# An MLP written out at both ends: the branch on odd weights first, eight PSUM banks, the last output layer tile by tile

## What is computed

```python
def _tlin(x, w, s): return jnp.einsum('bsi,oi->bso', x, w) * s   # w holds -1, 0 and 1
# x is 8 x 256 x 128; w1, w2: 512 x 128; h1, h2: 512 x 512; w3: 128 x 512
h = silu(_tlin(x, w1_w, w1_s)) * _tlin(x, w2_w, w2_s)
h = gelu(_tlin(h, h1_w, h1_s), approximate=False)
h = gelu(_tlin(h, h2_w, h2_s), approximate=False)
x = _layernorm(x + _tlin(h, w3_w, w3_s))
```

## Time and profile before

| what | value |
|---|---|
| three runs | 384.06, 384.48, 386.58 us; median 384.48 |
| the profiled execution | 384.94 us |
| its span, first to last instruction | 383.1 us |
| mean granted TensorE clock | 0.963 of full speed |
| TensorE busy | 334.1 us, 87% |
| DVE, ACT, POOL busy | 263.8, 210.9, 180.4 us |

### The profile page before, as it was taken

One profiled execution on the slowest core, in us unless ns is written; L12 is line 12 of the kernel. 1 busy time (PEld: TensorE's weight loads), 2 busy tenths in 40 slices (PEclk: granted clock), 3 DMA queues, 4 the chain that ended last, 5 costly groups with the idle time before them and its releaser, 6 DMA issues.

```text
span 383.1 us, 8611 instructions
## 1 busy us (share of the span) xinstructions
PE 334.1 (87%) x2572; PEld 305.8 (80%) x2572; DVE 263.8 (69%) x849; ACT 210.9 (55%) x429; POOL 180.4 (47%) x242
## 2 busy tenths in 40 slices
PE   3798899976857999999967999999688999999991
PEld 1798788866747999988856888888588999999890
DVE  3767877866853578678863989887865777666641
ACT  2457556624522455455466878875357666767330
POOL 0033777655472447975687666643133333233300
PEclk9999999976896999999998999999999999999997
DMA  8980001021232625223303000000000000000000
GB/s 270 432 331 0 23 29 37 31 62 35 56 79 71 199 58 169 56 62 86 109 24 125 0 2 2 1 3 2 1 2 3 0 15 15 14 14 3 27 14 17
DMA packets 17033, 23.71 MB, mean 62 GB/s; under 512 B 3424, under 2 KB 14176, under 8 KB 16208
## 3 DMA queue, kind: packets, MB, share of 16 engines
q1 hardware_dynamic: 13712, 17.97, 14.3%
q0 software_dynamic: 2272, 4.69, 3.7%
q10 hardware_dynamic: 1008, 0.53, 0.5%
HBM read 17.45 MB, written 6.73 MB: 63 GB/s over the span
## 4 chain that ended last, share of the span: by engine, by line
PE 61%; DVE 9%; issue 8%; POOL 4%; ACT 3%; another core or an unknown queue 2%; POOLq 0%; DVEq 0%; ACTq 0%
PE ps L1902 8%; PE ps L1903 8%; PE ps L1539 7%; PE ps L1541 6%; PE ps L1540 6%; PE ps L1739 5%; PE ps L1943 3%; PE ps L1847 3%; PE ps L1728 2%; PE ps L1862 2%; PE ps L1622 1%; POOL sb_w_lo L568 1%; ACT sb_stage L724 1%; PE ps L1874 1%
## 5 line engine op out<-in xcount | busy, mean ns | idle before, releaser
L1902 PE MATMUL ps<-sb_w_hi,sb_fh_hi 128*128 128x256 f32 x256 | 63.5, 286 | 0.9 <-POOL sb_w_lo L596 0.8
L1903 PE MATMUL ps<-sb_w_lo,sb_fh_hi 128*128 128x256 f32 x256 | 62.7, 283 | 0.0
L1902 PEld LDWEIGHTS ps<-sb_w_hi,sb_fh_hi 128*128 128x128 f32 x256 | 49.0, 191 | 1.3 <-POOL sb_w_lo L596 1.0
L1903 PEld LDWEIGHTS ps<-sb_w_lo,sb_fh_hi 128*128 128x128 f32 x256 | 49.0, 191 | 0.0
L596 POOL TENSOR_TENSOR sb_w_lo<-sb_x_in,sb_w_hi 128x256 fp32r<-128x256 f32 x32 | 23.3, 759 | 43.2 <-DVE sb_w_hi L1484 43.2
L448 POOL DMA_INDIRECT routed<-sb_rows_of,sb_row x32 | 31.8, 993 | 17.6 <-issue 9.1
L1739 PE MATMUL ps<-sb_w,sb_stage 128*128 x234 | 34.1, 284 | 3.9 <-ACT sb_xT_in L730 3.0
L1539 PE MATMUL ps<-sb_w_hi,sb_rT_hi 128*128 x78 | 30.6, 392 | 7.2 <-issue 5.0
L1739 PEld LDWEIGHTS ps<-sb_w,sb_stage 128*128 128x128 f32 x234 | 30.2, 197 | 4.6 <-issue 4.5
L547 POOL DMA_INDIRECT answers<-sb_stage x24 | 25.0, 1043 | 12.3 <-issue 7.7
L568 POOL TENSOR_TENSOR sb_w_lo<-sb_x_in,sb_w_hi 128x512 fp32r<-128x512 f32 x16 | 20.7, 1294 | 19.9 <-DVE sb_w_hi L1365 19.8
(11 more groups left out here) (303 smaller groups left out, 1053.1 us busy)
## 6 DMA issues: line engine op xcount, KB each, us to landing
sb_stage<-in_w SPq DMA_DIRECT2D x2, 1408.0 KB, 13.3
sb_stage<-routed SPq DMA_DIRECT2D x24, 65.0 KB
sb_w<-in_w SPq DMA_DIRECT2D x1, 1536.0 KB, 17.9
sb_x_in<-in_x_tok SPq DMA_DIRECT2D x1, 1024.0 KB, 8.9
sb_x_in<-in_ff_h SPq DMA_DIRECT2D x1, 1024.0 KB
sb_xT_in<-in_ff_h SPq DMA_DIRECT2D x1, 1024.0 KB
sb_got_first<-answers SPq DMA_DIRECT2D x4, 256.0 KB, 3.2
sb_w<-answers SPq DMA_DIRECT2D x4, 256.0 KB, 3.5
```

What stands on the lines that cost most here:

```text
L1902: mm(dst, w_hi, x_hi, start=start, stop=False)
L1903: last = mm(dst, w_hi, x_lo, start=False, stop=stop and exact)
```

## The change

- TensorE reads the odd-weight number and branches ahead of the MLP's first product. Both branches hold the whole MLP (`mlp(exact)`). The waits for `st`, `x2T` and `qp` of all batches come ahead of it as well.
- The first layer of batch 0 uses banks 1, 2, 6 and 7, so that no tile waits for another, and its second layer banks 4 to 7, one tile in each. `f_silu` has four places.
- TensorE's opening is one list: the whole first layer of batch 0, then `attention_rows(7)`, the first layer of batch 1 around `x3_transposes(6)`, the second layer of batch 0, and so on. On DVE the product and the casts of batch 0 come ahead of `x3_moments(7)`, and the splits of its Gelu ahead of `low_x3(7)`.
- In batches 0 and 7 the low parts of tiles 2 and 3 move from POOL to DVE (`shared_low_parts`). POOL's `x3_root(7)` comes behind its two low parts of batch 0.
- ACT touches Silu once at the end of the attention, ahead of `high_x3(5)`.
- The closing is written out on TensorE and ACT. The split Gelu of batch 7 has rooms of its own (`g_rooms`), so it doesn't wait for the third layer of batch 6; the output layer of batch 6 comes behind the first tile of the third layer of batch 7; the last output layer runs over `k` outside and tokens inside, in banks 0 and 1, and waits for one tile of Gelu at a time.

Rooms and banks:

```diff
-        f_silu = work[:, 0, :].rearrange("p (m t) -> p m t", t=SEQ)
+        f_silu = work[:, 0:2, :].rearrange("p n (m t) -> p (n m) t", t=SEQ)
...
+        def g_rooms(b):
+            return (x3T_hi[:, 0:FF_TILES, :], x3T_lo[:, 0:FF_TILES, :]) if isinstance(b, int) and b == BATCHES - 1 else (g_hi, g_lo)
...
-        in_bank = (1, 2, 3, 1)
+        in_bank, opening_bank = (1, 2, 3, 1), (1, 2, 6, 7)
...
+        def second_bank(b, m):
+            return ps[:, 4 + m, 0:SEQ] if isinstance(b, int) and b == 0 else half_bank(4, m)
```

POOL:

```diff
-                    for m in range(FF_TILES):
+                    for m in range(FF_TILES // 2 if isinstance(i, int) and i in (0, BATCHES - 1) else FF_TILES):
...
-            attention(attention_step, first=5, end=ATTENTION_STEPS + 2)
+            attention(attention_step, first=5, end=ATTENTION_STEPS + 1)
             mlp_rest(0)
+            x3_root(7)
             mlp_rest(1)
-            steps(pool, BATCHES, MLP_LAG, mlp_rest, first=EARLY)
+            steps(pool, BATCHES, MLP_LAG, mlp_rest, ahead=1, first=EARLY)
```

ACT:

```diff
+            nc.scalar.activation(touched[:, :], ones[:, 0:1], ACT.Silu)
             high_x3(5)
             mlp_first(0)
             mlp_rest(0)
+            mlp_first(1, (0, 1))
             high_x3(6)
-            mlp_first(1)
+            mlp_first(1, (2,))
+            mlp_rest(1)
             high_x3(7)
-            mlp_rest(1)
-            steps(act, BATCHES, MLP_LAG, mlp_step, first=EARLY)
+            mlp_first(1, (3,))
+            steps(act, BATCHES, MLP_LAG, mlp_step, first=EARLY, left=3)
+            third_gelu(6, (0, 1))
+            second_gelu(7, (0, 1))
+            second_gelu(7, (2, 3))
+            third_gelu(6, (2, 3))
+            third_gelu(7, range(FF_TILES))
```

DVE:

```diff
+            def shared_low_parts(b):
+                for m in range(FF_TILES // 2, FF_TILES):
+                    dve.wait_ge(ff["a_hi"], FF_TILES * b + m + 1)
+                    V.tensor_tensor(a_lo[:, m, :], f_a[:, m, :], a_hi[:, m, :].bitcast(fp32), ALU.subtract).then_inc(ff["a_lo"], 1)
...
             mlp_first(0, (0, 1))
             x3_residual(7)
+            mlp_first(0, (2, 3))
+            high_parts_of_first(0)
+            shared_low_parts(0)
             x3_moments(7)
-            mlp_first(0, (2, 3))
+            mlp_first(1, (0, 1))
             low_x3(6)
-            mlp_rest(0)
+            mlp_first(1, (2,))
             x3_norm(7)
-            mlp_first(1)
+            low_parts_of_second(0)
             low_x3(7)
-            mlp_rest(1)
-            steps(dve, BATCHES, MLP_LAG, mlp_step, first=EARLY)
+            mlp_first(1, (3,))
+            high_parts_of_first(1)
+            steps(dve, BATCHES, MLP_LAG, mlp_step, ahead=1, first=EARLY)
```

TensorE:

```diff
             def output_layer(b):
+                wait(pe, ff["res"], b)
+                if isinstance(b, int) and b == BATCHES - 1:
+                    for k in range(FF_TILES):
+                        pe.wait_ge(ff["g2"], FF_TILES * b + k + 1)
+                        for t in range(TILES):
+                            last = mm(ps[:, t, 0:D], f_last[:, k, t * P:(t + 1) * P], ff_out_w[:, k, :],
+                                      start=k == 0, stop=k == FF_TILES - 1)
...
-            mlp_ready()
-            first_layer(0, (0, 1), False)
-            attention_rows(7)
-            x3_transposes(6)
-            pe.wait_ge(at["res3"], BATCHES)
-            first_layer(0, (2,), False)
-            mlp_rest(0)
-            mlp_first(1)
-            x3_transposes(7)
-            mlp_rest(1)
+            def mlp(exact):
+                mlp_ready()
+                first_layer(0, range(FF_TILES), exact)
+                attention_rows(7)
+                first_layer(1, (0, 1), exact)
+                x3_transposes(6)
+                pe.wait_ge(at["res3"], BATCHES)
+                first_layer(1, (2,), exact)
+                second_layer(0, (0, 1), exact)
+                first_layer(1, (FF_TILES - 1,), exact)
+                second_layer(0, (2, 3), exact)
+                x3_transposes(7)
+                third_layer(0, (0, 1), exact)
+                first_layer(2, range(FF_TILES), exact)
+                second_layer(1, (0, 1), exact)
+                third_layer(0, (2, 3), exact)
+                second_layer(1, (2, 3), exact)
+                steps(pe, BATCHES, MLP_LAG, lambda i: mlp_step(i, exact), first=MLP_LAG, left=3)
+                output_layer(5)
+                third_layer(6, (0, 1), exact)
+                second_layer(7, (0, 1), exact)
+                second_layer(7, (2, 3), exact)
+                third_layer(6, (2, 3), exact)
+                third_layer(7, (0,), exact)
+                output_layer(6)
+                third_layer(7, (1, 2, 3), exact)
+                output_layer(7)
...
             with pe.If(n_odd == 0):
-                steps(pe, BATCHES, MLP_LAG, lambda i: mlp_step(i, True), first=EARLY)
+                mlp(True)
             with pe.Else():
-                steps(pe, BATCHES, MLP_LAG, lambda i: mlp_step(i, False), first=EARLY)
+                mlp(False)
```

More of the change, by code:

```diff
@@ L812, in attention_step, with mlp_first @@
                 query_exps(s - 4)
-            def mlp_first(i):
+            def mlp_first(i, tiles=range(FF_TILES)):
                 if isinstance(i, int) and i == 0:
@@ L819, in mlp_first @@
                     act.wait_ge(at["x2"], BATCHES)
-                for m in range(FF_TILES):
+                    act.wait_ge(at["lo"], BATCHES)
+                    act.wait_ge(at["v_tok"], BATCHES)
+                for m in tiles:
                     if live(i, BATCHES):
@@ L823, in mlp_first, with third_gelu @@
                         act.wait_ge(ff["in_mm"], n + 1)
-                        wait(act, ff["act"], n - 1)
-                        nc.scalar.activation(f_silu[:, m % 2, :], ps[:, in_bank[m], 0:SEQ], ACT.Silu,
+                        wait(act, ff["act"], n - FF_TILES + 1)
+                        nc.scalar.activation(f_silu[:, m, :], ps[:, first_bank(i, m), 0:SEQ], ACT.Silu,
                                              scale=ff_s[:, 0, m:m + 1]).then_inc(ff["silu"], 1)
+            def third_gelu(b, tiles):
+                if live(b, BATCHES):
+                    for m in tiles:
+                        act.wait_ge(ff["h2_mm"], FF_TILES * b + m + 1)
+                        wait(act, ff["out_mm"], b)
+                        nc.scalar.activation(f_last[:, m, :], half_bank(6, m), ACT.Gelu,
+                                             scale=ff_s[:, 3, m:m + 1]).then_inc(ff["g2"], 1)
@@ L828, in mlp_rest, with second_gelu @@
+            def second_gelu(b, tiles):
+                if live(b, BATCHES):
+                    for m in tiles:
+                        n = FF_TILES * b + m
+                        act.wait_ge(ff["h1_mm"], n + 1)
+                        wait(act, ff["g_lo"], n - FF_TILES + 1)
+                        nc.scalar.activation(f_g[:, m, :], second_bank(b, m), ACT.Gelu,
+                                             scale=ff_s[:, 2, m:m + 1]).then_inc(ff["g1"], 1)
             def mlp_rest(i):
                 for pair in range(0, FF_TILES, 2):
-                    b = i - 2
@@ L831, in mlp_rest @@
[L831 to L844, removed]
+                    third_gelu(i - 2, (pair, pair + 1))
@@ L846, in mlp_step @@
+                    second_gelu(i - 1, (pair, pair + 1))
             def mlp_step(i):
@@ L1471, in mlp_rest, with low_parts_of_second @@
                     normalise(f_out, f_res, mv, rstd, TILES, D, ff["out"])
-                b = i - 1
+                low_parts_of_second(i - 1)
+                high_parts_of_first(i)
+                if isinstance(i, int) and i == BATCHES - 1:
+                    shared_low_parts(i)
+            def low_parts_of_second(b):
                 for m in range(FF_TILES):
@@ L1909, in first_layer, with square_layer @@
                     n = FF_TILES * i + m
-                    wait(pe, ff["act"], (n, n - 3, n - 3, n - 2)[m])
+                    if not isinstance(i, int) or i > 0:
+                        wait(pe, ff["act"], (1 if isinstance(i, int) and i == 1 else n, n - 3, n - 3, n - 2)[m])
                     for w in range(2):
                         rows = slice(m * P, (m + 1) * P)
-                        last = mlp_product(ps[:, in_bank[m], w * SEQ:(w + 1) * SEQ], fi_hi[:, w, rows], fi_lo[:, w, rows],
+                        last = mlp_product(ps[:, first_bank(i, m), w * SEQ:(w + 1) * SEQ], fi_hi[:, w, rows], fi_lo[:, w, rows],
                                            x3T_hi[:, i, :], x3T_lo[:, i, :], True, True, exact)
                     last.then_inc(ff["in_mm"], 1)
-            def square_layer(layer, b, tiles, bank, x_hi, x_lo, ready, read, done, exact):
+            def square_layer(layer, b, tiles, x_hi, x_lo, ready, read, done, exact):
                 if not live(b, BATCHES):
@@ L1923, in square_layer @@
                     rows = slice(m * P, (m + 1) * P)
```

(9 more changed lines are left out.)

30 lines of the change are left out of this document (16 added, 14 removed).

## The result

Over 20 runs of each, the median went from 386.1 to 380.7 us (377.6 to 384.2). The ratio is 0.9876, with a 95% interval of 0.9849 to 0.9903: 1.2% faster, 4.8 us (3.7 to 5.8). It leaves out the runs of either kernel that fell in a slower state, which the medians of all 20 include: these differ by 5.4 us. The forecast was 4.1 us less.

What follows compares the result with a forecast made beforehand. TensorE alone bounds the MLP's steady part, so only its opening and closing can gain, the opening being set by DVE's order. 4.3 + 1.3 - 1.5 = 4.1 us off 384.48 gives 380.4 us, range 378.4 to 382.6.

Steps and rivals of the forecast that it cites:

- The opening, 4.3 us: From the MLP's first product to step 3: step 3 starts at 294.9 in place of 299.2, 4.3 us gained.
- Nearly all of the gain is the third products: Opening: removing 32 products at 0.12 us saves 3.8 us of TensorE; waits sum to no less than before.
- The low parts, 2.75 us from the first cast: Batch 0's casts and low parts, shared by DVE and POOL, take 2.75 us in place of 3.3.
- The rival in which they shut each other out wholly: DVE's casts and parts exclude POOL's: 3.8 us instead of 2.75, 1.0 more at both ends, 382.4; chance 0.15.
- The closing, 1.3 us: End of the MLP: earlier low parts of batch 7 and no wait before the last output layer, 1.3 us gained.
- The term of the last output layer: Closing: 12 of 16 passes cover the last Gelu, so a wait of 0.7 us goes.
- the low parts' 0.55: Closing: batch 7's casts and low parts take 2.75 for 3.3, so its second layer starts 0.55 us earlier.
- The clock, 1.5 us lost: Opening: TensorE's new 2.7 us wait drops the granted clock to 0.50, costing 1.5 us, bounds 0 to 3.0.
- The full-clock rival: The clock holds in the opening despite the long wait: 378.9 us; chance 0.22.
- The branch, nothing: Branch ahead of the MLP's first product: cost 0 to 0.3 us, taken as 0 because hidden behind short products.
- The fetch rival: Branch at the entry and TensorE's loop back edges wait for instruction fetch: 10 us cost, 390; chance 0.04.
- Banks and the Silu table, nothing: Opening: extra banks, four Silu places and the early Silu table get no value, since DVE is waited for.

Runs made afterwards that it cites:

- the version without POOL: Changed kernel with all four low parts of batches 0 and 7 on DVE, none on POOL: ratio 0.9828 to the kernel before, 0.9858 when run again.
- second and third execution of the changed kernel: The changed kernel unaltered, timed and profiled twice more: ratios 0.9879 and 0.9856 to the kernel before.
- the wait filled: Changed kernel plus 14 products nobody reads, in TensorE's longest wait of the opening, ahead of batch 0's second layer: ratio 0.9877 to the kernel before.
- the third products back: Changed kernel with the 32 third products of batches 0 and 1 put back, order and banks as changed: ratio 0.9932 to the kernel before.
- seven banks: Changed kernel with bank 1 again for tile 3 of batch 0's first layer, which then waits for DVE's first product: ratio 0.9859 to the kernel before.

## Why the prediction was right, and where not

- **The number:** that 380.7 stands so near the forecast of 380.4 is in part luck. The forecast counts down from the three runs' 384.48, and over 20 runs the kernel before took 386.1. What can be compared is the gain, 4.1 forecast and 4.8 measured.
- **The opening, 4.3 us:** measured 4.22 in the first profile, and these steps of the walk lie within 0.2 us of the trace, relative to the first product: second layer of batch 0 at 7.57 against 7.7, third layer at 13.48 against 13.6, step 3 at 24.67 against 24.6. It held because each step was taken from DVE's order, which has no freedom.
- **"Nearly all of the gain is the third products":** wrong. The waits did sum to about the same before and after (5.8 and 5.2), and 32 x 0.12 is 3.8, but equal sums don't mean that each product removed was on the path: 14 of the 32 lay in waits. Put back they cost 2.16 us, and removed alone they let waits grow. The order earned the other half.
- **The low parts, 2.75 us from the first cast:** 2.82 measured, for a different reason. The step took the casts at 2.00, stretched by POOL, and DVE's parts as the last. In the first profile DVE ran through (0.89, and 0.75 for its parts), and POOL's first part, begun 0.36 behind the first cast as before, took 1.78 in place of 0.74 and ended behind all of DVE's; the second took 0.72. In the closing it was the other way round: casts 2.00, POOL 1.49 for two, DVE last, 2.67 us in all. Both orders end at about the same time, which is why the number stood; that is luck.
- **The rival in which they shut each other out wholly** had 3.8, and neither end took so long. But its price was wrong, and the mechanism is near to what the rows show: it charged each cast 0.36, the lag of POOL's start, while casts that follow each other take 0.20 each (0.89 for four, with overlap). Wholly in turn the work is 4 x 0.20 + 2 x 0.74 + 2 x 0.34 = 3.0, against the 2.82 and 2.67 measured. The argument against it, 4.4 against 3.3 in the kernel before, becomes 3.8 against 3.3: still less than wholly in turn, but no longer far from it.
- **The rule on shared ports** of the Trainium skill, SBUF — State Buffer, section "SBUF: two separate sides", says that the blocked side waits out the whole instruction. POOL's first part here, 1.78, and DVE's third cast there, 0.85, which ended 0.15 behind the POOL part it met, agree with it, as does the version without POOL, in which nothing is stretched (0.90 and 1.43). In the opening POOL waited out more than one instruction: it ended behind the last of DVE's unbroken run. The rule speaks for giving all parts to one engine, a step that the prediction didn't take.
- **The closing, 1.3 us:** 1.48 to 1.50 measured. The term of the last output layer was 0.7 and measured 0.82 (1.48 less 0.66 for the low parts); the low parts' 0.55 measured 0.66, by which the second layer of batch 7 starts earlier, counted from the first product of step 3.
- **The clock, 1.5 us lost:** its size was right, 1.50 us when it fell. That it falls was taken for likely and is so in some executions only. The full-clock rival (378.9) describes the first profile, the forecast the second; the measured 4.8 us lies between their 5.6 and 4.1, and its interval holds both.
- **The branch, nothing:** right. The fetch rival did not occur; the branch at the entry took 0.09 us, the loop's back edges at most 0.24, and only the one at the end of the body took 3.59, hidden as before.
- **Banks and the Silu table, nothing:** right for the table; bank 7 for tile 3 is worth 0.2 us on DVE. The four places for Silu and the second layer's four banks were not undone by themselves.

## What to carry to other kernels

Work taken off the busiest engine is worth only what of it lies outside that engine's waits: walk the order step by step from the engine that is late, and check the walk by putting the work back. Before one short job is halved between two engines, measure it whole on one of them, and look in the trace at each instruction and not at the mean: here DVE alone had casts and low parts ready in 2.3 us, with two parts on POOL it took 2.7 to 2.9, and with all four on POOL 3.3 to 3.6. When a part of a kernel is changed, compare stages from a common instruction: here the nearly unchanged part ahead of the MLP moved by 2.4 us between two executions, half of the gain.

## What was not expected

- A tightened schedule can lose its gain to the clock. The branch moved alone took 2.7 us (worked out) of waiting and products out of stage 1 and gave 1.5 back in the profiled execution by a granted clock of 0.50; the whole kernel's time did not move measurably.
- With the same waits of 2.3 us the clock fell in some executions and held in others. What decides between them stays open.
- In the opening POOL's first subtraction of 128x256 took 1.78 us and DVE's four casts 0.89; in the closing of the same execution POOL's took 0.74 and the casts 2.00. Both times POOL began 0.36 us behind the first cast. In the opening it was POOL, too, in the second and third execution of the changed kernel, with the wait filled, with the closing undone and without the touch of Silu, but DVE with the third products back and with seven banks. What decides it stays open.
